# Two transformer layers on one core: casts, norm squares and the last quantisation products move to GpSimd, max parts are packed, and the PSUM banks are divided anew

## What is computed

```python
xn = layernorm(x)
x = x + cosine_attention(xn) + (softmax_attention(xn) + top2_of_8_experts(xn))
xn = layernorm(x)
x = x + causal_attention(xn) + fp4_gated_mlp(xn)
```

## Time and profile before

| | us |
|---|---|
| median of 3 runs (lowest, highest) | 2050.38 (2048.84, 2050.67) |
| the profiled execution, its own time | 2050.03 |
| its span, first to last instruction | 2048.2 |
| busy in the span: ScalarE | 1875.9 |
| busy in the span: VectorE | 1790.3 |
| busy in the span: TensorE, products | 1625.1 |
| busy in the span: GpSimd | 1062.5 |

### The profile page before, as it was taken

How to read it: one execution, slowest core, us unless ns; L and a number is a source line. 1 busy time by engine, 2 the same in 40 slices (tenths; PEclk the granted TensorE clock), 3 DMA queues, 4 the chain that set the end, 5 groups by cost and what they waited for, 6 DMA issues and landing times.

```text
span 2048.2 us, 39684 instructions
## 1 busy us (share of the span) xinstructions
PE 1625.1 (79%) x12405; PEld 796.0 (39%) x12405; DVE 1790.3 (87%) x4071; ACT 1875.9 (92%) x2144; POOL 1062.5 (52%) x448
## 2 busy tenths in 40 slices
PE   2678788888888888888888888888888888887865
PEld 1233444433444443344444334444433444443433
DVE  5778989999998999999899999989999998998844
ACT  2399999999999999999999999999999999999991
POOL 1455555456555545655554565555456555545520
PEclk9979999999999999999999999999999999999875
DMA  1000000000000000000000000000000000000000
GB/s 41 4 4 1 6 6 0 5 6 5 6 5 6 0 5 6 5 6 5 6 0 5 6 5 6 5 6 0 5 6 5 6 5 6 0 5 7 4 4 6
DMA packets 21059, 11.21 MB, mean 5 GB/s; under 512 B 1431, under 2 KB 20953, under 8 KB 20956
## 3 DMA queue, kind: packets, MB, share of 16 engines
q1 hardware_dynamic: 20956, 10.20, 1.7%
HBM read 6.00 MB, written 4.19 MB: 5 GB/s over the span
## 4 chain that ended last, share of the span: by engine, by line
ACT 40%; DVE 23%; issue 22%; PE 13%; POOL 1%; DVEq 1%; ACTq 1%; SPq 0%; DMA 0%; POOLq 0%
ACT curve L532 21%; ACT root L532 7%; ACT prob L532 3%; PE psM L1167 3%; DVE nmax L858 3%; DVE curve L848 3%; PE psM L1004 2%; ACT L563 2%; ACT L636 1%; PE psV L1199 1%; DVE h L421 1%; ACT hqT L532 1%; POOL qk L514 1%; PE psM L1151 1%; DVE hqT L417 1%
## 5 line engine op out<-in xcount | busy, mean ns | idle before, releaser
L532 ACT ACTIVATE curve<-curve 128x2048 f32<-128x2048 f32 x384 | 717.7, 1902 | 4.8 <-POOL curve L503 3.4
L500 POOL TENSOR_TENSOR root<-curve 128x2048 f32<-128x2048 f32 x128 | 460.1, 3600 | 426.1 <-DVE curve L852 425.9
L532 ACT ACTIVATE root<-root 128x2048 f32<-128x2048 f32 x256 | 484.4, 1905 | 8.1 <-POOL root L500 7.8
L503 POOL TENSOR_TENSOR curve<-curve,root 128x2048 f32<-128x2048 f32 x64 | 348.8, 5452 | 93.3 <-ACT root L532 93.3
L852 DVE TENSOR_SCALAR curve<-psS 128x1024 f32<-128x1024 f32 x256 | 306.0, 1216 | 25.3 <-PE psS L1035 19.1
L858 DVE TENSOR_REDUCE nmax<-psS 128x4 f32<-128x1024 f32 x256 | 308.8, 1214 | 7.2 <-PE psS L1044 6.9
L1199 PE MATMUL psV<-prob,vf 128*32 128x256 f32 x2048 | 270.8, 425 | 3.9 <-ACT prob L532 0.6
L532 ACT ACTIVATE prob<-psS 128x1024 f32<-128x1024 f32 x256 | 261.3, 1021 | 11.8 <-PE psS L1065 11.0
L1199 PE MATMUL psV<-curve,vc 128*32 128x256 f32 x2048 | 225.4, 408 | 40.0 <-ACT curve L532 36.3
L520 POOL TENSOR_TENSOR stk<-qk,stk 128x512 f16<-128x512 f32 x128 | 168.4, 1325 | 155.3 <-ACT stk L532 155.3
L848 DVE TENSOR_TENSOR curve<-curve,root 128x2048 f32<-128x2048 f32 x64 | 177.7, 2777 | 5.6 <-ACT root L532 5.6
(11 more groups left out here) (190 smaller groups left out, 2856.9 us busy)
## 6 DMA issues: line engine op xcount, KB each, us to landing
xt<-in_L_attn_x SPq DMA_DIRECT2D x32, 128.0 KB, 2.2
out<-yo SPq DMA_DIRECT2D x32, 128.0 KB, 1.8
we<-in_L_ffn_W_experts SPq DMA_DIRECT2D x1, 512.0 KB
curve<-in_L_attn_w_qkv SPq DMA_DIRECT2D x1, 192.0 KB
curve<-in_L_ffn_w_down SPq DMA_DIRECT2D x1, 176.0 KB
curve<-in_L_ffn_w_gate SPq DMA_DIRECT2D x2, 64.0 KB
curve<-in_L_ffn_w_up SPq DMA_DIRECT2D x2, 64.0 KB
curve<-in_L_ffn_W_qkv SPq DMA_DIRECT2D x1, 128.0 KB
```

The costliest lines, as they stand in the source:

```text
L500: nc.gpsimd.tensor_tensor(root[:, two], curve[:, p, two], curve[:, p, two], ALU.mult).then_inc(s_sq, 1)
L503: nc.gpsimd.tensor_tensor(curve[:, p, two], curve[:, p, two], root[:, two], ALU.mult).then_inc(s_half[0], 1)
L532: return nc.scalar.activation(out, in_, func, **kw)
```

## The change

- `high` (a cast by a copy), the square of `norm`, and step 8 of `quantx` and `quanth` run on GpSimd; ScalarE's and VectorE's parts of them are gone. Ahead of each cast GpSimd does an addition of one column (`carry`).
- The parts of the maxima are packed: a row's 16 heads times 3 parts (and a zero) fill 128 columns in place of 512, so `maxT` does 2 transposes in place of 8, and copies 256 columns in place of 1024. A constant `pickb`, made in the setup by two VectorE instructions, selects a head's parts in `e` in place of `onesb`.
- `psV` is one bank that both products with v share; `pvw` of a batch waits for `oF` of the same batch, `pvf` for `oC` of the batch before. `psM` has three banks.
- `SCHEDULE` is another order, with some lags changed: all of `m` and the first `experts` have lag 1, all of `c` lag 0, `oF` and `residual` lag 0, `s1e` and `p1T` lag -2, `quanth` 0 and 1 lag -1.
- Instructions on the big score tiles keep their width of 2048.

```diff
+MISC_BANKS = 3
...
 SCHEDULE = [
-    ("table", 0, -1), ("wln", 0, -1), ("c", 1, 0), ("sq", 0, 0), ("fadd", 0, -1), ("pvf", 7, -1), ("oF", 0, -1),
-    ("m", 4, 0), ("wexp", 0, -1), ("ln0", 0, 1), ("experts", 0, 0), ("wln", 1, -1), ("c", 2, 0), ("c", 3, 0),
-    ("o1", 0, -2), ("wexp", 1, -1), ("finf", 0, -1), ("pvw", 0, -1), ("wln", 2, -1), ("c", 4, 0), ("m", 5, 0),
-    ("wln", 3, -1), ("pvw", 1, -1), ("c", 5, 0), ("wexp", 2, -1), ("quanth", 0, -2), ("pvw", 2, -1), ("wexp", 3, -1),
-    ("ln", 0, 0), ("m", 6, 0), ("experts", 1, 0), ("pvw", 3, -1), ("sq", 1, 0), ("sq", 2, 0), ("m", 7, 0),
-    ("pvw", 4, -1), ("sq", 3, 0), ("rstd0", 0, 1), ("stack", 0, 1), ("pvw", 5, -1), ("quanth", 1, -2), ("load", 0, 1),
-    ("unit", 0, 1), ("ln", 1, 0), ("oC", 0, -1), ("pvw", 6, -1), ("pvw", 7, -1), ("xnT", 0, 1), ("maxT", 0, 0),
-    ("quanth", 2, -2), ("quanth", 3, -2), ("c", 6, 0), ("c", 7, 0), ("proj", 0, 1), ("finc", 0, -1), ("stack", 1, 1),
-    ("ln", 2, 0), ("e", 0, 0), ("proj", 1, 1), ("norm", 0, 1), ("ocT", 0, -1), ("e", 1, 0), ("high", 0, 1),
-    ("w1", 0, -2), ("wo", 0, -1), ("stack", 2, 1), ("e", 2, 0), ("pvf", 0, 0), ("pvf", 1, 0), ("pvf", 2, 0),
-    ("ln1", 0, -1), ("ln", 3, 0), ("quanth", 4, -2), ("rstd1", 0, -1), ("xn1T", 0, -1), ("guess", 0, 1),
-    ("gexp", 0, 1), ("quantx", 0, -1), ("quanth", 5, -2), ("gmax", 0, 1), ("stack", 3, 1), ("quanth", 6, -2),
-    ("newton", 0, 1), ("e", 3, 0), ("quantx", 1, -1), ("choose", 0, 1), ("p1", 0, -1), ("high", 1, 1), ("e", 4, 0),
-    ("high", 2, 1), ("quanth", 7, -2), ("s1", 0, -1), ("choose", 1, 1), ("e", 5, 0), ("quantx", 2, -1), ("pvf", 3, 0),
-    ("s1e", 0, -1), ("e", 6, 0), ("high", 3, 1), ("quanth", 8, -2), ("quantx", 3, -1), ("residual", 0, 1),
-    ("quantx", 4, -1), ("choose", 2, 1), ("pvf", 4, 0), ("e", 7, 0), ("quantx", 5, -1), ("table", 1, 0),
-    ("stackT", 0, 1), ("stackT", 1, 1), ("sigm", 0, 0), ("quantx", 6, -1), ("stackT", 2, 1), ("quantx", 7, -1),
-    ("hT", 0, -2), ("choose", 3, 1), ("sigm", 1, 0), ("quantx", 8, -1), ("m", 0, 1), ("stackT", 3, 1), ("mul", 0, 0),
-    ("m", 1, 1), ("hT", 1, -2), ("xqT", 0, -1), ("m", 2, 1), ("mul", 1, 0), ("sigm", 2, 0), ("gu", 0, -1),
-    ("pvf", 5, 0), ("hmul", 0, -1), ("rs1", 0, -1), ("m", 3, 1), ("arctan", 0, 0), ("sigm", 3, 0), ("c", 0, 1),
-    ("pvf", 6, 0), ("down", 0, -2), ("mul", 2, 0), ("arctan", 1, 0), ("p1T", 0, -1), ("choose", 4, 1), ("mul", 3, 0),
-    ("arctan", 2, 0), ("gu", 1, -1), ("arctan", 3, 0), ("choose", 5, 1), ("hmul", 1, -1),
+    ("table", 0, -1), ("wln", 0, -1), ("wexp", 0, -1), ("c", 0, 0), ("s1e", 0, -2), ("wln", 1, -1), ("pvw", 0, -1),
+    ("wln", 2, -1), ("c", 1, 0), ("wexp", 1, -1), ("wexp", 2, -1), ("pvw", 1, -1), ("wln", 3, -1), ("p1T", 0, -2),
+    ("c", 2, 0), ("residual", 0, 0), ("sq", 0, 0), ("sq", 1, 0), ("quanth", 2, -2), ("ln0", 0, 1), ("c", 3, 0),
+    ("wexp", 3, -1), ("quanth", 3, -2), ("c", 4, 0), ("experts", 1, 0), ("pvw", 2, -1), ("rstd0", 0, 1),
+    ("pvw", 3, -1), ("pvw", 4, -1), ("pvw", 5, -1), ("ln", 0, 0), ("o1", 0, -2), ("pvw", 6, -1), ("maxT", 0, 0),
+    ("quanth", 4, -2), ("quanth", 5, -2), ("oC", 0, -1), ("pvw", 7, -1), ("xnT", 0, 1), ("quanth", 6, -2),
+    ("quanth", 7, -2), ("ln", 1, 0), ("c", 5, 0), ("c", 6, 0), ("quanth", 8, -2), ("proj", 0, 1), ("rs1", 0, -2),
+    ("proj", 1, 1), ("finc", 0, -1), ("gmax", 0, 1), ("e", 0, 0), ("finf", 0, -1), ("e", 1, 0), ("c", 7, 0),
+    ("sq", 2, 0), ("gexp", 0, 1), ("ocT", 0, -1), ("pvf", 0, 0), ("norm", 0, 1), ("ln", 2, 0), ("e", 2, 0),
+    ("w1", 0, -2), ("wo", 0, -1), ("e", 3, 0), ("choose", 0, 1), ("high", 0, 1), ("guess", 0, 1), ("pvf", 1, 0),
+    ("ln1", 0, -1), ("fadd", 0, -1), ("e", 4, 0), ("choose", 1, 1), ("high", 1, 1), ("rstd1", 0, -1), ("pvf", 2, 0),
+    ("pvf", 3, 0), ("ln", 3, 0), ("e", 5, 0), ("e", 6, 0), ("choose", 2, 1), ("xn1T", 0, -1), ("quantx", 0, -1),
+    ("stack", 0, 1), ("pvf", 4, 0), ("newton", 0, 1), ("e", 7, 0), ("quantx", 1, -1), ("quantx", 2, -1),
+    ("quantx", 3, -1), ("stackT", 0, 1), ("stackT", 1, 1), ("sq", 3, 0), ("table", 1, 0), ("unit", 0, 1),
+    ("load", 0, 1), ("quantx", 4, -1), ("choose", 3, 1), ("sigm", 0, 0), ("stack", 1, 1), ("quantx", 5, -1),
+    ("choose", 4, 1), ("hT", 0, -2), ("quantx", 6, -1), ("quantx", 7, -1), ("high", 2, 1), ("pvf", 5, 0),
+    ("stack", 2, 1), ("m", 0, 1), ("hT", 1, -2), ("sigm", 1, 0), ("quantx", 8, -1), ("m", 1, 1), ("mul", 0, 0),
+    ("stackT", 2, 1), ("p1", 0, -1), ("m", 2, 1), ("xqT", 0, -1), ("mul", 1, 0), ("sigm", 2, 0), ("gu", 0, -1),
+    ("mul", 2, 0), ("hmul", 0, -1), ("arctan", 0, 0), ("m", 3, 1), ("s1", 0, -1), ("hmul", 1, -1), ("sigm", 3, 0),
+    ("mul", 3, 0), ("gu", 1, -1), ("arctan", 1, 0), ("high", 3, 1), ("m", 4, 1), ("quanth", 0, -1), ("pvf", 6, 0),
+    ("pvf", 7, 0), ("arctan", 2, 0), ("down", 0, -2), ("m", 5, 1), ("choose", 5, 1), ("stack", 3, 1),
+    ("stackT", 3, 1), ("oF", 0, 0), ("m", 6, 1), ("m", 7, 1), ("experts", 0, 1), ("arctan", 3, 0), ("quanth", 1, -1),
 ]
...
-        mstk = sb("mstk", [P, NT, HEADS, FULL_GROUP], BF16)
-        mT = sb("mT", [P, 4, T], BF16)
+        mstk = sb("mstk", [P, NT, 4, FULL_GROUP], BF16)
+        mT = sb("mT", [P, T], BF16)
+        pick = sb("pick", [P, 8])
+        pickb = sb("pickb", [P, 4, P], BF16)
...
-        psV = psum("psV", [P, 2, 2, T])
-        psM = [psum(f"psM{k}", [P, 512]) for k in range(2)]
+        psV = psum("psV", [P, 2, T])
+        psM = [psum(f"psM{k}", [P, 512]) for k in range(MISC_BANKS)]
...
-            return psM[n % 2], n % 2
+            return psM[n % MISC_BANKS], n % MISC_BANKS
...
-                ins = nc.vector.tensor_tensor(o, n, bc(a, 2, BLOCK), ALU.mult)
+                ins = eng.tensor_tensor(o, n, bc(a, 2, BLOCK), ALU.mult)
...
+            def carry(k):
+
+                nc.gpsimd.tensor_tensor(holdp[:, k:k + 1], iota8[:, 0:1], iota8[:, 0:1], ALU.add)
...
+                if stage == "norm":
+                    pool.wait_ge(s_nsum, due(s_nsum, b - 1))
+                    pool.wait_ge(s_qkc, due(s_qkc, b))
+                    cos = qk[:, 0:2, :, :, :].rearrange("p k j h d -> p (k j h) d")
+                    nc.gpsimd.tensor_tensor(qsq[:, :, :], cos, cos, ALU.mult).then_inc(s_qsq, 1)
+                if stage == "high":
+
+                    kind = KINDS[arg]
+                    src, hi, lo = stack_parts(kind)
+                    pool.wait_ge(s_qkf, due(s_qkf, b))
+                    if kind < 2:
+                        pool.wait_ge(s_stkq, due(s_stkq, b))
+                    pool.wait_ge(s_stkTp, due(s_stkTp, b - 1, arg + 1))
+                    carry(kind)
+                    nc.gpsimd.tensor_copy(hi, src).then_inc(s_stk1, 1)
...
+                if stage == "quantx" and arg == FP4_STEPS - 1:
+                    fp4(pool, xn1[:, :, :].rearrange("p j d -> p (j d)"), xq1[:, :, :].rearrange("p j d -> p (j d)"),
+                        (qxa, qxr, qxe), s_qx, b, arg)
+                if stage == "quanth" and arg == FP4_STEPS - 1:
+                    fp4(pool, h[:, :, :].rearrange("p j n -> p (j n)"), h[:, :, :].rearrange("p j n -> p (j n)"),
+                        (qa, qr, qe), s_qh, b, arg)
...
-                if stage == "norm":
-                    act.wait_ge(s_nsum, due(s_nsum, b - 1))
-                    act.wait_ge(s_qkc, due(s_qkc, b))
-                    activate(qsq[:, :, :], qk[:, 0:2, :, :, :].rearrange("p k j h d -> p (k j h) d"),
-                             ACT.Square).then_inc(s_qsq, 1)
...
-                if stage == "high":
-
-                    kind = KINDS[arg]
-                    src, hi, lo = stack_parts(kind)
-                    act.wait_ge(s_qkf, due(s_qkf, b))
-                    if kind < 2:
-                        act.wait_ge(s_stkq, due(s_stkq, b))
-                    act.wait_ge(s_stkTp, due(s_stkTp, b - 1, arg + 1))
-                    activate(hi, src, ACT.Copy).then_inc(s_stk1, 1)
...
-                    activate(oCs[:, :, :], psV[:, 0, :, :], ACT.Copy).then_inc(s_oC, 1)
+                    activate(oCs[:, :, :], psV[:, :, :], ACT.Copy).then_inc(s_oC, 1)
...
-                    activate(mT[:, :, :], bankb[k], ACT.Copy).then_inc(s_mT, 1)
+                    activate(mT[:, :], bankb[k][:, 0, :], ACT.Copy).then_inc(s_mT, 1)
...
+            link(nc.vector.tensor_reduce(pick[:, :], ident[:, :].rearrange("p (h g c) -> p g h c", h=4, c=4), AX.XY, ALU.add))
+            link(nc.vector.tensor_copy(pickb[:, :, :], bc(pick[:, 0:4], 2, P)))
...
+                    def part(c):
+                        return mstk[:, :, :, 0:16].rearrange("p j h (g c) -> p j g h c", c=4)[:, :, :, :, c]
+
+                    top_score = nmax[:, :, :].rearrange("p j (g h) -> p j g h", h=4)
+                    rest = nres[:, :, :].rearrange("p j (g h) -> p j g h", h=4)
+                    link(nc.vector.tensor_copy(part(0), top_score))
+                    link(nc.vector.tensor_tensor(rest, top_score, part(0), ALU.subtract))
+                    link(nc.vector.tensor_copy(part(1), rest))
```

(20 more changed lines are left out.)

15 lines of the change are left out of this document (6 added, 9 removed).

## The result

The kernel after took 2078.95 us (median of 4 runs, 2076.73 to 2083.16), the kernel before beside it 2050.32. The ratio is 1.0143, with a 95% interval of 1.0126 to 1.0161: slower, where 1962 was forecast.

A forecast was written before the change was run, and what follows sets the result against it. ScalarE's own work was taken as the old bound, GpSimd's chain as the new one: period 57.4 us, 75 us less in 31 periods, 13 less in fill and drain, hence 1962 us; range 1920 to 2012.

The forecast's parts named there:

- ScalarE's floor: ScalarE's busy time per period after losing casts, a square and most of the max copy: 57.8 - 3.3 = 54.5 us.
- The chain from `quanth` 7 to stack 1: GpSimd's queue holding up VectorE's stackT 1: 16.9 us with transposes and hand-overs, closing the cycle at 57.2 us.
- Fill and drain: Setup, start and end of the span, outside the steady periods: -13 us in sum, between 0 and -20.
- VectorE's wait at `stackT`: Expected sign: a VectorE copy of stackT waits 3 to 4 us for TensorE once per period.
- TensorE "at nothing": Six of eight bf16 transposes go and a third bank helps; with 9 us of slack per period, gain put at nothing.
- contention at 0.2 us: GpSimd and VectorE slowing each other on two SBUF operands: 0.2 us added per cycle, bounds 0 and 1.5.
- Rival 3: Full blocking of VectorE by running GpSimd instructions: 2.3 us per period, period 59.7, total 2033 us; chance 0.04.
- the bound is ScalarE's own work: Old kernel's steady period: ScalarE busy 57.80 of 59.82 us, 1.8 idle, VectorE 3 us behind; both must shorten.
- the 3.3 us: ScalarE's saving per period: four casts, one square and most of the max copy, 4 x 0.53 + 0.53 + 0.64.
- Rival 5: Moved parts speed nothing since ScalarE wasn't the bound; excluded because its idle time was 1.8 us, no chance given.
- Rivals 1 and 2: Shorter GpSimd chain, period 55.7, 1910 us, chance 0.10; stacked waits on ScalarE, period 59.5, 2035 us, chance 0.12.
- Rival 4: Slow strided fp16 casts on GpSimd: at 2.8 us each, period 61.5 and total 2089 us; chance 0.06.

The follow-up runs named there:

- Filler: Kernel after plus 56 transposes of a constant that compute nothing, ahead of TensorE's wait for stack 3: 2005.07 us, 0.9784 of the kernel before.
- warm_wait: Kernel after plus 24 transposes of a constant ahead of TensorE's wait for stack 3: 2027.18 us, 0.9912 of the kernel before.
- before_packed: Kernel before with nothing but the packed maxima (2 transposes for 8, copy of 256 columns for 1024): 2060.69 us, ratio 1.0055.
- sq3_on_act_warm: Kernel after plus 56 constant transposes, with sq 3 moved from GpSimd to ScalarE as a Square before ln 3: 2035.93 us, 0.9929 of the kernel before.

## Why the prediction was wrong

**Right.** ScalarE's floor (54.5 forecast, 54.88 in the period shown), GpSimd's sum (40; 40.21), the prices of the norm square (1.07; 1.04), `quanth` 8 (1.45; 1.387) and the cast (0.75; 0.639 mean, 0.607 median). The Trainium skill ("GPSIMD Engine Reference", section "Engine selection") calls one-input work on GpSimd roughly line rate. The estimate drawn from it was 0.43 us plus dispatch; with 0.18 us for the dispatch, the shortest one-column operation of this trace, that is 0.61, and the measured cast agrees. The chain from `quanth` 7 to stack 1, on the timelines of VectorE and GpSimd:

```profile
1004.02 0.89 DVE L427 SCALAR_TENSOR_TENSOR h<-hqT,h 128x704 f32<-128x704 f32 x1
...
1020.13 1.07 POOL L522 TENSOR_TENSOR qk<-qk,rn 128x512 f32<-128x512 f32 x1 [2.44 <-DVE rn L810]
1021.16 1.34 POOL L543 TENSOR_TENSOR stk<-qk,stk 128x512 f16<-128x512 f32 x1
```

It took 1022.50 - 1004.91 = 17.6 us where I had 16.3 without the transposes, with a wait of 2.44 us for `newton` that I hadn't counted in. Fill and drain gave 17 us, in the range of 0 to 20. But the chain isn't what closes the period: VectorE's wait at `stackT` was 42.9 us in all, 1.3 a batch, not 3 to 4. Two slips in the working: the earlier trace rows is 1.05 us a period, not nearly all of 1.8; and half of 2 x 1.2 + 2 x 1.6 is 2.8, not the 1.5 given as the bound of contention.

**First failed step, the largest: TensorE "at nothing".** I gave it 9 us of slack and asked only whether work would go. Its order had a price: of the entries behind stack 1 I wrote that they come "about when they are due", and listed high 2, stack 2, quantx 8 and two products. High 3 and stack 3, behind `mul` 2, were not in that list, though a stage of TensorE waits for them. The price was not the stall of 3.42 us itself but the clock behind it: at the lower level the experts took 3.1 us a period longer, and VectorE, which gathers them, waited 81.4 us for them in place of 25.4. Filler showed this: 2.49 us of the 3.87, and two neighbouring periods of `warm_wait`, with the same idle time and unlike clocks, differ by as much.

**Second: contention at 0.2 us, the lock dismissed.** I wrote that "the trace doesn't bear it out", since line 423 was never lengthened by over 0.56 us. But an operation is lengthened by what is *left* of the other engine's instruction when it starts, and a fixed order brings it in at nearly the same point each time: the earlier trace rows showed one such point, no bound., with 2276 to 4499 ns, spoke for the lock. I also looked for victims among the large operations; the new ones are 2 and 64 elements wide. Line 758 alone adds (739 - 150) x 2 = 1.2 us to VectorE per batch, which is most of why its busy time didn't fall (53.4 forecast, 55.26). Line 501 took 0.64 in place of 0.10 for the same reason. The Trainium skill ("SBUF — State Buffer", section "SBUF: two separate sides") calls this port pair an exclusive lock held for the whole instruction. The runs agree: 2.9 us more on an operation of 0.2, 2.5 more on one of 0.9, 4.3 behind a `mul` of 4.5. Rival 3, its consequence, got 0.04, and its averaging (so many starts, half a unit each) was also wrong: what is hit depends on the order, and each reordering hit something else.

**Third: "the bound is ScalarE's own work".** Busy 57.8 of 59.6 us with 1.8 idle looked like a bound by sum. `before_packed` took 0.64 us away and won nothing, even where TensorE kept its clock: the copy had stood in the shadow of proj's products, so this term of the 3.3 us was worth nothing in the kernel before. Rival 5, "excluded", shouldn't have been. What the rest of ScalarE's work is worth wasn't tried alone; adding 1.8 us, with holds on VectorE removed, cost 1.07 (`sq3_on_act_warm`). TensorE's six transposes, "at nothing" too, are a candidate for what keeps the clock up in the kernel before.

**Rivals 1 and 2** (55.7 us, and a gain used up by waits on ScalarE at 59.5) didn't come: ScalarE waited 19.0 us for oC in all, 0.6 a batch, not up to 2. **Rival 4**, the only one on the slower side, had its number (2089) near the result and its cause wrong: the casts cost 0.64, not 2.8.

**Open.** With the 56 transposes the period is 58.78, 1.38 above the forecast. VectorE is busy 440.47 / 8 = 55.1 us in it, 1.7 over its floor. `sq3_on_act_warm` brought that to 429.49 / 8 = 53.7, so the holds by `sq` 3 make up most of it (line 758 takes 217 ns there); but there ScalarE's added work took the time, and no edit here removes the holds without loading another engine or hitting another operation. That the lock is the 1.38 us is argued, not shown. A kernel with the casts on GpSimd and without `carry` wasn't tried.

## What to carry to other kernels

Before moving work to GpSimd, go through its queue entry by entry and ask of each, the last one too, which engine stops for it and what VectorE runs beside it: a VectorE operation with two operands in SBUF, and in one case here one with a single operand (line 798), can wait out the rest of a GpSimd instruction, however small it is. When TensorE has slack, look at where it stands idle and what comes next; a stall of 3 us ahead of heavy products is worth filling with useless ones, but only if the granted clock shows a loss there. A busiest engine with 97% busy time isn't proof of a bound; take a little off it alone, look at what it waits for in that place, and compare periods in which TensorE's clock is the same.

## What was unexpected of the hardware

- A vector operation on 2 or 64 elements per partition (0.15 to 0.2 us) took up to 1.6 and 3.1 us beside a GpSimd unit of 3.6, and a one-column addition on GpSimd took up to 2.26 us beside VectorE's `mul` of 2.3.
- 56 transposes that compute nothing took 3.3 us of TensorE per period and made the kernel 74 us faster than without them; the same 56 made the kernel before 54 us slower, and 90 of them gave back more than half of the gain.
- In one run, with equal idle time of TensorE ahead of the same products (1.89 and 1.90 us), they ran at the high clock in one period and partly at the lower one in its neighbour, and the periods were 58.8 and 61.3 us long.
